# A two-layer decoder kernel: the order of two softmax rounds in its text attention, filler matmuls, and the place of one load

## The reference

```python
vis = bitnet_linear(dinov2_features, W_d2v, b_d2v)
image_embeds = bitnet_linear(vis, W_img, b_img)
fused = bitnet_linear(text_embeddings, W_txt, b_txt)
for Wa, ba in ((W_att0, b_att0), (W_att1, b_att1)):
    kv = bitnet_linear(image_embeds, Wa, ba)
    k = jnp.concatenate([kv, kv], axis=-1)
    scores = jnp.einsum('bse,bpe->bsp', fused, k) * inv_sqrt_e
    attn = jax.nn.softmax(scores, axis=-1)
    fused = fused + 0.1 * jnp.einsum('bsp,bpe->bse', attn, k)
```

## Time and profile before

| | us |
|---|---|
| median of 3 runs | 1394.28 |
| lowest and highest | 1392.86, 1396.47 |
| the profiled execution | 1392.02 |
| its span | 1390.3 |
| first stage | 0 to 53.6 |
| text attention | 291.4 to 347.6 |

### The profile page before, as it was taken

How to read it: one execution, slowest core, us unless ns; L and a number is a source line. 1 busy time by engine, 2 the same in 40 slices (tenths; PEclk the granted TensorE clock), 3 DMA queues, 4 the chain that set the end, 5 groups by cost and what they waited for, 6 DMA issues and landing times. The chain is left out here.

```text
span 1390.3 us, 20427 instructions
## 1 busy us (share of the span) xinstructions
PE 1082.0 (78%) x6765; PEld 905.1 (65%) x6770; DVE 982.5 (71%) x1801; ACT 480.6 (35%) x1066; POOL 398.2 (29%) x541
## 2 busy tenths in 40 slices
PE   1588888765686599999415598898889889998987
PEld 1477777643265488888203387777777877787877
DVE  5689999855866012322199999999999999999510
ACT  0112112131063332222101164655545554655452
POOL 1112222100022400000400154635354443636353
PEclk9799999986787699999757699999999999999999
DMA  8015520000002866666270000000000000000000
GB/s 279 16 68 179 183 91 8 1 1 1 0 1 98 328 241 227 229 232 220 68 305 0 1 1 1 8 0 0 8 0 8 0 8 0 8 0 0 8 9 9
DMA packets 23972, 98.86 MB, mean 71 GB/s; under 512 B 3728, under 2 KB 15184, under 8 KB 17584
## 3 DMA queue, kind: packets, MB, share of 16 engines
q1 hardware_dynamic: 16080, 73.60, 14.4%
q10 hardware_dynamic: 5200, 17.37, 3.7%
q0 software_dynamic: 2640, 7.21, 1.5%
HBM read 87.96 MB, written 21.76 MB: 79 GB/s over the span
## 5 line engine op out<-in xcount | busy, mean ns | idle before, releaser
L1978 PE MATMUL bank<-n_hA_hi_reduced,ffn_h 128*128 128x256 f32 x512 | 130.8, 296 | 14.4 <-POOL n_hA_lo_reduced L1805 14.4
L1978 PE MATMUL bank<-n_hB_hi_reduced,ffn_h 128*128 128x256 f32 x512 | 125.8, 290 | 6.1 <-ACT n_hA_lo L2104 4.4
L1978 PE MATMUL bank<-n_hA_lo_reduced,ffn_h 128*128 128x256 f32 x512 | 127.2, 290 | 0.0
L1978 PE MATMUL bank<-n_hB_lo_reduced,ffn_h 128*128 128x256 f32 x512 | 120.3, 279 | 0.0
L1978 PEld LDWEIGHTS bank<-n_hA_hi_reduced,ffn_h 128*128 128x128 f32 x512 | 102.2, 200 | 17.8 <-POOL n_hA_lo_reduced L1805 17.2
L2216 DVE TENSOR_TENSOR d_prod<-d_qk,d_xT 128x512 f32<-128x512 f32 x128 | 105.2, 861 | 0.5
L1978 PEld LDWEIGHTS bank<-n_hB_hi_reduced,ffn_h 128*128 128x128 f32 x512 | 96.5, 189 | 9.5 <-ACT n_hA_lo L2104 5.8
L1978 PEld LDWEIGHTS bank<-n_hA_lo_reduced,ffn_h 128*128 128x128 f32 x512 | 102.5, 200 | 0.2
L1614 ACT ACTIVATE e_hT<-bank,e_b 128x128 f32<-128x128 f32 x184 | 52.6, 368 | 137.4 <-PE bank L1557 137.4
L1978 PEld LDWEIGHTS bank<-n_hB_lo_reduced,ffn_h 128*128 128x128 f32 x512 | 96.6, 189 | 1.8 <-issue 1.7
L1639 DVE TENSOR_TENSOR e_y<-bank,e_b 128x256 f32<-128x256 f32 x23 | 9.8, 424 | 123.9 <-PE bank L1569 123.9
(11 more groups left out here) (340 smaller groups left out, 2631.0 us busy)
## 6 DMA issues: line engine op xcount, KB each, us to landing
e_w<-in_W SPq DMA_DIRECT2D x23, 1024.0 KB, 5.0
ffn_weights<-in_F ACTq DMA_DIRECT2D x2, 5632.0 KB, 20.1
e_piece<-ffn_weights SPq DMA_DIRECT2D x11, 1024.0 KB, 4.9
ffn_h<-ffn_weights SPq DMA_DIRECT2D x2, 4096.0 KB, 18.7
ffn_w<-ffn_weights SPq DMA_DIRECT2D x3, 1024.0 KB, 7.0
expert_rows<-zero ACTq DMA_DIRECT2D x1, 2944.0 KB, 10.3
e_xs<-expert_rows SPq DMA_DIRECT2D x23, 128.0 KB, 4.5
expert_out<-e_y POOLq DMA_DIRECT2D x23, 128.0 KB, 2.0
```

Source lines behind the costliest of these rows:

```text
L1978: last = nc.tensor.matmul(F[f % 2][:, 0:PAIR], weight(w[:, k, f * P:(f + 1) * P], fast), operand(src[part][1][:, k, :], fast), start=(c == ...
```

## The change

- On SP the two DMAs of `wkv` move from ahead of `f1` to behind `f2`.
- In the text attention the order of the eight (stream, round) pairs becomes all four first rounds, then all four second rounds: `TURNS` and the hand-written orders of PE, ACT and VectorE follow it. `scores(3)` comes ahead of `second(1)`; `turned(3, 0)` and `second(2)`, `second(3)` ahead of `updates(0)`; VectorE takes `shifted(3, 0)` and `probabilities(3, 0)` ahead of `shifted(2, 1)`.
- `second` has one bank now, not two, and waits for `shifted(u - 1, 1)`.
- The bank that comes free is the target of `spare(n)`: n matmuls of the identity with 256 columns of the mask (bf16), whose result nobody reads. There are 8 ahead of the transpose of the maximum, 12 behind it, and groups of 2 to 4 between later steps, 43 in all.

```diff
             for n, (name, k, width, _) in enumerate(BITS):
-                if name == "f1":
-                    for c in range(KD):
-                        rows = slice(c * HALF_DC, (c + 1) * HALF_DC)
-                        sp.dma_start(wkv[0:HALF_DC, c, :], ins["wkv"][rows, :]).then_inc(wkv_loaded, 16)
                 if name == "d2v":
...
                     sp.dma_start(raw[name][:, :, :], ins["W_" + name]).then_inc(raw_loaded[n], 16)
+            for c in range(KD):
+                rows = slice(c * HALF_DC, (c + 1) * HALF_DC)
+                sp.dma_start(wkv[0:HALF_DC, c, :], ins["wkv"][rows, :]).then_inc(wkv_loaded, 16)
             sp.dma_start(m.wqkv[:, :, :], ins["wqkv0"]).then_inc(m.w0_loaded, 16)
...
-    text, score, bank_p, bank_g, upd = m.banks[0:2], m.banks[2:4], m.banks[4], m.banks[5:7], m.banks[7]
+    text, score, bank_p, bank_g, bank_w, upd = m.banks[0:2], m.banks[2:4], *m.banks[4:8]
...
-    TURNS = [(0, 0), (1, 0), (2, 0), (0, 1), (1, 1), (3, 0), (2, 1), (3, 1)]
+    TURNS = [(u, l) for l in range(2) for u in range(NU)]
...
             def second(u):
 
                 pe.wait_ge(probT_ready, TURNS.index((u, 0)) + 1)
-                if u >= 2:
-                    pe.wait_ge(sub_ready[u - 2], 2)
+                if u:
+                    pe.wait_ge(sub_ready[u - 1], 2)
...
+            def spare(n):
+
+                for _ in range(n):
+                    nc.tensor.matmul(bank_w[:, 0:256], m.identb[:, :], m.maskb[:, 0:4, :].rearrange("p t s -> p (t s)"),
+                                     start=True, stop=True)
+
+            spare(8)
             pe.wait_ge(amax_ready, 1)
             nc.tensor.transpose(bank_p[:, 0:P], col[:, 0:1].broadcast_to([P, P]), m.ident[:, :]).then_inc(amax_turned, 1)
+            spare(12)
             for u in range(2):
                 projected(u, 0)
                 projected(u, 1)
                 scores(u)
                 projected(u, 2)
+            spare(3)
             turned(0, 0)
...
             turned(1, 0)
             projected(3, 0)
             projected(3, 1)
+            scores(3)
+            projected(3, 2)
+            spare(2)
+            turned(2, 0)
             second(1)
-            projected(3, 2)
-            scores(3)
-            turned(2, 0)
+            spare(2)
+            turned(3, 0)
+            second(2)
+            spare(2)
             turned(0, 1)
-            second(2)
+            second(3)
+            spare(2)
+            turned(1, 1)
             updates(0)
-            turned(1, 1)
-            turned(3, 0)
-            second(3)
+            spare(4)
+            turned(2, 1)
             updates(1)
-            turned(2, 1)
+            spare(4)
+            turned(3, 1)
             updates(2)
-            turned(3, 1)
+            spare(4)
             updates(3)
...
             projected(1, 0)
+            exped(0, 0)
             projected(1, 1)
-            exped(0, 0)
...
             projected(2, 2)
+            copied(1, 0)
             exped(2, 0)
-            copied(1, 0)
             projected(3, 0)
             exped(0, 1)
             projected(3, 1)
             projected(3, 2)
             copied(2, 0)
+            exped(3, 0)
             exped(1, 1)
+            copied(3, 0)
             copied(0, 1)
             exped(2, 1)
-            exped(3, 0)
             copied(1, 1)
-            copied(3, 0)
+            exped(3, 1)
             copied(2, 1)
-            exped(3, 1)
             copied(3, 1)
...
             probabilities(2, 0)
+            shifted(3, 0)
             shifted(1, 1)
             probabilities(0, 1)
+            probabilities(3, 0)
             shifted(2, 1)
             probabilities(1, 1)
-            shifted(3, 0)
             updated(0)
-            probabilities(3, 0)
+            shifted(3, 1)
             probabilities(2, 1)
             updated(1)
-            shifted(3, 1)
+            probabilities(3, 1)
             updated(2)
-            probabilities(3, 1)
             updated(3)
```

More of the change, by code:

```diff
@@ L792, in second_of @@
     def second_of(u):
-        return bank_g[u % 2][:, 0:TQ * SC].rearrange("p (t s) -> p t s", t=TQ)
+        return bank_g[:, 0:TQ * SC].rearrange("p (t s) -> p t s", t=TQ)
     with nc.Block() as block:
@@ L834, in second @@
                 pe.wait_ge(probT_ready, TURNS.index((u, 0)) + 1)
-                if u >= 2:
-                    pe.wait_ge(sub_ready[u - 2], 2)
+                if u:
+                    pe.wait_ge(sub_ready[u - 1], 2)
                 for t in range(TQ):
-                    last = nc.tensor.matmul(bank_g[u % 2][:, t * SC:(t + 1) * SC], pT[u][0:SC, t * P:(t + 1) * P],
+                    last = nc.tensor.matmul(bank_g[:, t * SC:(t + 1) * SC], pT[u][0:SC, t * P:(t + 1) * P],
                                             m.cross01[:, u % B, :], start=True, stop=True)
```

## The result

| | before | changed |
|---|---|---|
| median of 22 runs, us | 1396.0 | 1399.66 |
| lowest, highest | 1392.36, 1398.79 | 1393.77, 1403.03 |
| ratio to before, 95% | | 1.0024 [1.0014, 1.0034] |
| the profiled execution, its span | 1392.02, 1390.3 | 1401.27, 1399.6 |

The change makes the kernel 3.4 us slower, 2.0 to 4.7 by the interval. The two profiled executions lie 9.3 us apart, so the changed kernel's profile is of one of its slower runs, and before's of one of its fastest.

What follows compares the result with a forecast made beforehand. Bound taken: a chain between PE, ACT and VectorE in the attention, VectorE's wait for sc in the first stage. First stage -2.9 plus attention +2.4 gave -0.5 us: median 1393.8 us, range 1389.0 to 1400.5.

Steps and rivals of the forecast that it cites:

- Part 1: First stage's loads: with wkv behind f1 and f2, small load sc lands earlier, -2.9 us, bounds -3.8 and +1.1.
- the sign for it: First stage's DMAs: a rate above 400 GB/s from 12 to 17 us was to show the earlier landing.
- rival (e): First stage: packets don't pair as read, sc lands when it does now; total 1396.7 us, chance 0.04.
- the pairing: First stage: packets of SP's and ACT's queues alternate one for one, so each small packet costs one large one.
- the mean of 18 large packets per engine: First stage: the small loads last for 18 large packets per DMA engine, 8.3 us in the new order against 11.2.
- Part 2: Attention's head: eight spares delay the transpose +0.7 us, an earlier full clock gives -1.1; net -0.4, bounds -0.4 and +1.2.
- Part 3: Attention up to the first update: the new order makes that update start 5.25 us later.
- clock term: Attention's middle: PE's gap ahead of turned(3,0) may cost the clock, 1.8 us at one in three, +0.6 us.
- Part 4: Attention's tail, first update to last maximum: shrinks from 25.2 to 22.2 us, with turned and updates at half clock.
- Rival (b): Attention: clock falls ahead of turned(3,0), head's spares bring no rise; attention +5.6, total 1397.0 us, chance 0.15.
- point of decision: Attention's middle: the clock falls once PE's idle gap ahead of turned(3,0) reaches 3.6 us.
- the attention's +2.4: Text attention: head, middle and tail together, clock term included, cost +2.4 us.

Runs made afterwards that it cites:

- own_sem: Kernel before, with bcol on its own semaphore so VectorE no longer waits for all nine small loads; median 1390.92 us, ratio 0.9972.
- attn_only: Changed kernel with wkv back in its old place, keeping the attention's new order and spares; median 1400.78 us, ratio 1.0024.
- after_own: Changed kernel with the separate bcol semaphore of own_sem; median 1390.91 us, ratio 0.9982.
- attn_no_spare: attn_only with all ten calls of spare removed, the new order alone; median 1401.53 us, ratio 1.0038.
- fill_middle: attn_only with 20 spares instead of 2 ahead of turned(3,0) alone; median 1392.97 us, ratio 0.9996.
- attn_filled: attn_only with 20 spares ahead of turned(3,0), 24 ahead of turned(2,1), 16 ahead of turned(3,1); median 1394.08 us, ratio 0.9982.
- filled_own: attn_filled with the bcol semaphore of own_sem and without the eight spares ahead of the maximum's transpose; median 1387.79 us, ratio 0.995.
- wkv_128: Kernel before, with wkv's two DMAs taking 128 rows into 128 partitions instead of 96, in the old place; one run, 1391.37 us.
- wkv_only_look: A second profile of the kernel of wkv_only; the execution took 1388.94 us.
- wkv_only: Kernel before, with only the two wkv DMAs moved behind f1 and f2; median 1393.7 us, ratio 0.9988.
- wkv_last: Kernel before, with the wkv DMAs moved behind f1, f2, wqkv and wo, ahead of x only; median 1393.32 us, ratio 0.999.

## Why the prediction was wrong

The three parts of the attention, in us, from the profiles. The head runs from VectorE's first instruction to the first scores' `shifted`, the middle from there to the first update, the tail to the end.

| kernel | head | middle | tail | attention |
|---|---|---|---|---|
| before | 7.05 | 22.58 | 25.21 | 54.84 |
| own_sem | 6.92 | 22.25 | 25.22 | 54.39 |
| predicted | 6.65 | 28.4 | 22.2 | 57.2 |
| changed | 7.23 | 33.15 | 20.95 | 61.33 |
| attn_only | 6.67 | 32.06 | 21.37 | 60.10 |
| after_own | 7.22 | 33.16 | 21.01 | 61.39 |
| attn_no_spare | 7.05 | 31.63 | 21.88 | 60.56 |
| fill_middle | 7.23 | 27.62 | 21.23 | 56.08 |
| attn_filled | 6.67 | 27.61 | 18.22 | 52.50 |
| filled_own | 6.13 | 27.61 | 19.68 | 53.42 |

The attention is also that of before in `wkv_128` (54.84), `wkv_only_look` (54.33), `wkv_only` (56.10) and `wkv_last` (56.11). In the last two the clock is 0.50 from 325.8 and 322.4 us to the end of the stage. So the new order with small groups of spares or none, 60.1 to 61.4 us, stands against 54.3 to 56.1.

- **Part 1, the step that failed.** "So `sc` lands 2.9 us earlier" is not so: L390 starts at 24.07, 24.23 and 22.08 us, on average 0.2 later than L391 with `wkv` in the old place. The missing 2.9 is most of the 3.9 us between the forecast of -0.5 and the measured +3.4. The rate, which was to be the sign for it, came out as forecast (459 and 411 GB/s), and so it was no sign for the landing. The landing stayed about where it was, as in rival (e), but not by its mechanism. Right were the pairing, the rate of either stretch, and that the load into 96 partitions is the slow one. Wrong was to cost the mean of 18 large packets per engine: the last small packets still had large ones to pair with beyond those (32, 10 and 2 small ones from 18 to 20, 20 to 22 and 22 to 23 us), and these are `wkv` in the new order. The 39 small packets from 20 to 22 us in the trace of before, which the view of the earlier trace rows gives for that stretch, would have warned. `wkv_last` bears this out: with no `wkv` beside the last small packets the wait ends at 20.14. The Trainium skill, SBUF — State Buffer, "Door 1: The DMA port swizzle", has 218 GB/s for partitions 0 to 63, which reach 8 of 16 ports; the rows for 96 partitions have 213 to 243. But by the same page partitions 64 to 95 reach the other eight, so it gives the direction and not this number. What the Trainium skill, DMA: Bandwidth & Descriptors, "Queues, rings and completion order", says of some 9 to 17 descriptors in a row isn't what the traces show, if a packet of the profile is one descriptor: equal counts over 16 engines, 149 beside 149, would not exclude such turns, but the last three small packets, one packet of `wkv` apart, do.
- **Part 2.** +0.2 and not -0.4, within its bounds. Eight spares took 1.86 us at half clock (0.95 expected) and moved VectorE's step from 0.59 to 2.11 us behind its first instruction, and the early clock gave 1.3 of that 1.5 back. `fill_middle` and `after_own` repeat this (7.23, 7.22). In `attn_only` and `attn_filled` PE still had full clock from the stage before for a part of the eight, which took 1.14 and 1.21 us, and the head is the 6.65 of the forecast to 0.02. So the term is right where the clock happens to be up at the stage's start.
- **Part 3, the step that failed in the attention.** The order of events came as forecast: with the clock held, `attn_filled` and `fill_middle` take 27.6 us, where the prediction had 27.8 without its clock term (22.6 + 5.25). But that term, 0.6, was a third of 1.8 for two groups of matmuls. The fall came in all four profiles of the new order with the small spares or none, and it lasted for five or six groups: 31.6 to 33.2 us. `fill_middle` prices it at 4.4 us in the stage and 4.0 (0.6 to 7.3) in the runs.
- **Part 4.** Right in kind, up to 1.3 us too long: 20.9 to 21.9 us against 22.2. The clock was back for a part of it (1.00 from 344 to 347 us in the changed kernel, and `turned(3,1)` at 346.17 takes 1.09 us).
- **Rival (b)** names the gap in which the clock fell, and its sum for the attention, +5.6, is near the 5.3 to 6.6 of the profiles. That its sum fits is luck: it has +1.2 at the head (measured -0.4 to +0.2), 1.8 for the fall in the middle (measured 3.8 to 5.3 over 27.8) and a tail 0.4 longer than forecast (measured 0.3 to 1.3 shorter). It was given 0.15. Its point of decision, an idle gap of 3.6 us, was too high: 3.11 us behind two spares were enough. Its sum, 1397.0, rested on the gain of part 1; without it, it is 1399.9 on the prediction's base.
- **Direction.** Forecast was no change with a small gain; the loss is 3.4 us and clear of the scatter. 1399.66 lies within the stated range, 5.9 us above the 1393.8; 1.7 of that is that before's median came out at 1396.0 and not 1394.28. By the runs the attention's +2.4 isn't refuted (`attn_only` 1.0 to 5.9); what fails there is the sum inside it.

What stays open: the profiles give the attention 4.0 to 7.1 us more, the runs of `attn_only` 3.4 (1.0 to 5.9) and the changed kernel 3.4 (2.0 to 4.7). The old order alone varies by 1.8 us, with its clock. The stages behind the attention take 1038.9 to 1048.4 us in the profiles of kernels that don't differ there. Over a whole execution the granted clock goes with the time: the three of the changed kernel's 22 runs below 1395 us have 0.904 to 0.906, the others 0.895 to 0.904. In which stage such runs differ isn't known. If the half clock in the attention is avoided in some executions, the profiles were not among them; no run shows it.

## What to carry to other kernels

When steps in a chain of engines are reordered, list the new idle gaps of PE and price the clock for every group behind the gap until PE has recovered, not for the next one or two (five or six groups and 4.4 us here, where four were listed, two priced, and these at one in three). A gap can be filled: 20 matmuls of 0.12 us without a reader gave back 4.4 us in the stage, while the groups of two to four didn't hold the clock. A wait for a set of loads ends with its slowest packet, so split the semaphore by what is needed first before moving transfers around (3.9 us here, for a few lines).

## What was not expected of the hardware

- PE was busy without a gap from 320.8 to 333.2 us and was granted half clock all the time, 12.4 us. In `attn_filled` the same groups, with the same work, were at full clock. So a PE that is busy by the row can stay at half clock; what brought the clock back isn't known from these runs.
- While a load of 96 rows into 96 partitions was in flight, the DMAs moved 213 to 243 GB/s, the packets of `f1` beside it included; with 128 rows of the same tensor into 128 partitions they moved 426 to 448.
- The wait for one small load ended 2 us apart in two executions of one kernel (22.1 and 24.2 us).
